# Second experts of an audio tower: routing weights of chunks 2 to 7 spread by DMA, sums turned whole, first products a chunk ahead

## The reference

```python
logits = tokens @ router_w.T
rw, re = top_k(softmax(logits), 2)
rw = rw / maximum(rw.sum(-1, keepdims=True), 1e-12)
combine = zeros((N, E)).at[arange(N)[:, None], re].set(rw)
out = tokens
for e in range(8):
    h = gelu(tokens @ w1[e] + b1[e], approximate=False)
    out = out + combine[:, e:e + 1] * (h @ w2[e] + b2[e])
```

## Time and profile before

| | |
|---|---|
| median of 3 runs | 734.57 us (733.91 to 736.68) |
| the profiled execution | 732.55 us, its span 730.8 us |
| mean granted TensorE clock | 0.954 of full |
| PE busy | 635.5 us (87%) |
| DVE busy | 569.5 us (78%) |
| ACT busy | 502.0 us (69%) |
| POOL busy | 346.1 us (47%) |
| DMA | 24.36 MB, mean 33 GB/s |

### The profile page before, as it was taken

How to read it: one execution, slowest core, us unless ns; L and a number is a source line. 1 busy time by engine, 2 the same in 40 slices (tenths; PEclk the granted TensorE clock), 3 DMA queues, 4 the chain that set the end, 5 groups by cost and what they waited for, 6 DMA issues and landing times.

```text
span 730.8 us, 16309 instructions
## 1 busy us (share of the span) xinstructions
PE 635.5 (87%) x4928; PEld 348.6 (48%) x4928; DVE 569.5 (78%) x1627; ACT 502.0 (69%) x1264; POOL 346.1 (47%) x431
## 2 busy tenths in 40 slices
PE   5527998999999998999999996799888988879896
PEld 5514665665666654222222224555555655554332
DVE  6676787777777784889999989679988888857653
ACT  3747877888888873667777777567777777745542
POOL 1006678778788785433444455625445644320000
PEclk9858999999999998999999998699999999987999
DMA  4030000000000000533333330000000000000011
GB/s 112 1 115 1 1 2 1 0 0 0 0 0 0 0 1 24 185 116 117 118 115 117 117 118 1 2 1 2 0 0 1 0 0 0 1 1 2 15 22 22
DMA packets 22421, 24.36 MB, mean 33 GB/s; under 512 B 12390, under 2 KB 13414, under 8 KB 22118
## 3 DMA queue, kind: packets, MB, share of 16 engines
q1 hardware_dynamic: 20135, 23.31, 10.3%
q10 hardware_dynamic: 2239, 0.49, 0.4%
HBM read 22.48 MB, written 1.31 MB: 33 GB/s over the span
## 4 chain that ended last, share of the span: by engine, by line
PE 54%; DVE 25%; issue 9%; ACT 3%; POOL 2%; DMA 1%; DVEq 0%; SPq 0%; ACTq 0%; POOLq 0%
PE ps L726 8%; PE ps L762 8%; DVE big L1103 5%; PE ps L1581 5%; PE ps L1603 4%; PE ps L720 4%; DVE big L2093 3%; DVE big L1144 2%; PE ps L644 2%; PE ps L1587 2%; PE ps L655 2%; PE ps L708 2%; PE ps L712 2%; DVE big L1053 2%; PE ps L1836 2%
## 5 line engine op out<-in xcount | busy, mean ns | idle before, releaser
L1358 POOL TENSOR_TENSOR big<-big 128x1024 f32<-128x1024 f32 x64 | 119.9, 1895 | 44.1 <-DVE big L1164 44.1
L942 ACT ACTIVATE big<-ps,big 128x255 f32<-128x255 f32 x256 | 117.3, 485 | 11.4 <-DVE big L1158 8.9
L904 ACT ACTIVATE big<-ps,b1s 128x512 f32<-128x512 f32 x128 | 80.8, 683 | 33.3 <-PE ps L644 32.2
L1158 DVE TENSOR_REDUCE big<-ps 128x4 f32<-128x1020 f32 x64 | 75.1, 1213 | 26.6 <-PE ps L720 26.6
L1953 ACT ACTIVATE big<-ps 128x1024 f32<-128x1024 f32 x64 | 65.9, 1030 | 33.9 <-PE ps L1593 31.6
L2093 DVE TENSOR_REDUCE big<-ps 128x4 f32<-128x1020 f32 x64 | 78.1, 1220 | 6.8 <-DVE res L2150 2.5
L726 PE MATMUL ps<-cst,big 128*128 128x128 f32 x512 | 76.7, 283 | 6.3 <-POOL big L1358 2.4
L1170 DVE COPY mid<-ps 128x512 f32<-128x512 f32 x96 | 63.4, 685 | 18.3 <-PE ps L726 15.1
L726 PEld LDWEIGHTS ps<-cst,big 128*128 128x128 f32 x512 | 54.2, 140 | 40.8 <-issue 20.4
L644 PE MATMUL ps<-big,wall 64*128 64x512 f32 x256 | 73.1, 648 | 0.4 <-ACT big L875 0.4
L655 PE MATMUL ps<-big,w2s 128*64 128x512 f32 x256 | 70.8, 631 | 1.7 <-DVE big L1144 1.3
(11 more groups left out here) (277 smaller groups left out, 1310.6 us busy)
## 6 DMA issues: line engine op xcount, KB each, us to landing
mid<-spread_w SPq DMA_DIRECT2D x128, 128.0 KB, 2.9
mid<-in_split_sel SPq DMA_DIRECT2D x1, 1536.0 KB, 7.3
wall<-in_w SPq DMA_DIRECT2D x1, 1280.0 KB, 6.3
out_tokens<-res SPq DMA_DIRECT2D x16, 56.0 KB, 1.6
cst<-in_consts SPq DMA_DIRECT2D x1, 520.5 KB, 4.8
pexp<-in_w_raw SPq DMA_DIRECT2D x1, 512.0 KB, 5.8
w2s<-in_w SPq DMA_DIRECT2D x1, 512.0 KB, 3.2
mid<-in_taps ACTq DMA_DIRECT2D x1, 320.0 KB, 3.8
```

The source lines that it names most:

```text
L904: last = nc.scalar.activation(hid[e % 2][j], H1(e, j), ACT.Relu, bias=b1s[0][:, 2 * e + j:2 * e + j + 1])
L942: last = nc.scalar.activation(e_sb[r % 4][:, jj, tq, 0:NW], S[:, 2 * (r % 2) + jj, tq, 0:NW], ACT.Exp, scale=-1.0, bias=minus[r % 4][:, jj ...
L1158: nc.vector.tensor_reduce(minus[r % 4], S[:, 2 * a:2 * a + 2, :, 0:NW], AX.X, ALU.min).then_inc(s_mx, 1)
L1358: nc.gpsimd.tensor_tensor(e_sb[r % 4], e_sb[r % 4], bc(inverse[r % 4].unsqueeze(3), [P, 2, 2, 256]), ALU.mult).then_inc(s_A, 1)
```

## The change

- The first products run one chunk ahead: `hid` gets a second set of four buffers, PE's list becomes `hidden(c+1, 1)`, [`spread(c, 0)`], `second(c-1, 1)`, `hidden(c+2, 0)`, [`spread(c, 1)`], `sum_turn(c-1)`, `second(c, 0)`, and ACT's list follows it.
- `spread` on PE stays for chunks 0 and 1 only. For the others the combined table of a half (not its bf16 parts) is turned by one PE transpose (`combine_turn`), copied by ACT (`combine_out`), written to DRAM by SP (64 KB) and read back with two DMAs of 512 KB a chunk into `by_dma`, two buffers. `spread(c)` for c from 4 on waits until both weighings of chunk `c - 2` are done. `weigh` then reads both operands from SBUF.
- `sum_turn` is four plain transposes; `finish` adds the two halves, one each in two DVE operations. The tokens are added to `res` beforehand by POOL (`tokens_added`, eight operations of 128x256).
- The exponential of half 1 is a POOL power with base e of 128x16 in place of an ACT exponential (which needed two table loads).
- `combine` is split in `where`, `shares`, `combine` and `split`. Chunk 0 is taken first, then chunks 1 to 3, whose split comes after `weigh(0, 0)`. DVE's order around it changes too: `slot(B // 2, 2)` and `(B // 2, 5)` move behind that split, `rank(4)`, `best(6)` and `weigh(1, 0)` ahead of `slot(B // 2 + 1, 1)`, `rank(5)` and `slot(B // 2 + 1, 2)`.
- SP's stores are written out in place of a loop, each behind a `spread` of a later chunk for chunks 0 to 3.

The core of the diff (indentation cut by twelve):

```diff
+comb_turned = [big[:, 11008 + P * n:11008 + P * n + P] for n in range(2)]
+BY_PE = 2
+by_dma = [pos_t[:, 4 * n:4 * n + 4].rearrange("p k c q -> p k (c q)") for n in range(2)]
+there = [spread_w[2 * n:2 * n + 2].rearrange("c e q -> (c e) q") for n in range(2)]
+COMB_TURNED = lambda n: ps[:, 7 - 2 * n, 0:P]
...
-hid = [mo[:, 512 * n:512 * n + 512] for n in range(4)]
+hid = [mo[:, 512 * n:512 * n + 512] for n in range(4)] + [mid[:, 1024 + 512 * n:1536 + 512 * n] for n in range(4)]
...
+base = tail[:, 0:half]
...
+s_comb, s_cwp, s_cw, s_there = e0.s_comb, e0.s_ctp, e0.s_ct, e0.s_cd
+s_by_dma, s_pre = [sem(f"e1_spread{n}") for n in range(2)], sem("e1_tokens_added")
...
     def weights(d):
...
-        pe.wait_ge(s_c3, d // 4 + 1)
-        if d < 2:
+        pe.wait_ge(s_c3, 1 if d == 0 else 2 if d < 4 else 3)
+        if d == 0:
             pe.wait_ge(s_otr, B)
+        elif d == 2:
+            pe.wait_ge(s_fin, B)
+        elif d == 6:
+            pe.wait_ge(s_cw, CH + 2)
         for k in range(TC):
             last = nc.tensor.transpose(turned_weights(d)[:, P * k:P * k + P], c3[:, TC * d + k].rearrange("p r s -> p (r s)"), ident_b[:])
         last.then_inc(s_ctp, 1)
+    def combine_turn(n):
+        pe.wait_ge(s_comb, CH + n + 1)
+        if n == 0:
+            pe.wait_ge(s_ct, 1)
+        else:
+            pe.wait_ge(s_wgt, GROUPS * BY_PE)
+        nc.tensor.transpose(COMB_TURNED(n), comb_rows[n], ident).then_inc(s_cwp, 1)
     def hidden(c, g):
...
     def spread(c, g):
...
         s = GROUPS * c + g
-        pe.wait_ge(s_ct, 2 if s < 2 else 4 if s < 7 else CH)
+        pe.wait_ge(s_ct, c + 1)
         if s == 0:
             pe.wait_ge(s_lc, 6)
-        if s >= 1:
+        else:
             pe.wait_ge(s_wgt, s)
...
         s = GROUPS * c + g
+        if s == 0:
+            pe.wait_ge(s_ct, 4)
         if g == 0 and c >= 1:
             pe.wait_ge(s_ysb, c)
+        if g == 0:
+            pe.wait_ge(s_ct, 4 if c < 4 else CH)
         pe.wait_ge(s_wgt, s + 1)
...
-            last = nc.tensor.matmul(YT[:, D * k:D * k + D], y_sb[:, P * k:P * k + P], fold[:], start=True, stop=True)
+            last = nc.tensor.transpose(YT[:, P * k:P * k + P], y_sb[:, P * k:P * k + P], ident)
...
     hidden(0, 0)
-    for d in range(2):
-        weights(d)
+    hidden(0, 1)
+    hidden(1, 0)
+    weights(0)
+    hidden(1, 1)
     for c in range(CH):
-        hidden(c, 1)
+        if 1 <= c < CH - 1:
+            hidden(c + 1, 1)
+        if c < BY_PE:
+            spread(c, 0)
         if c == 0:
-            pe.wait_ge(s_fin, B)
-            for d in range(2, 4):
+            combine_turn(0)
+            for d in range(1, 4):
                 weights(d)
-        spread(c, 0)
         if c >= 1:
             second(c - 1, 1)
         if c < 2:
             x_turn(6 + c)
         if c == 3:
-            pe.wait_ge(s_wgt, GROUPS * c + 1)
             for d in range(4, CH):
                 weights(d)
-        if c < CH - 1:
-            hidden(c + 1, 0)
+        if c < CH - 2:
+            hidden(c + 2, 0)
         if c < 2:
             logits(6 + c)
-        spread(c, 1)
+        if c < BY_PE:
+            spread(c, 1)
+        if c == 2:
+            combine_turn(1)
         if c >= 1:
             sum_turn(c - 1)
-        if c == 0:
-            pe.wait_ge(s_ct, 4)
         second(c, 0)
     second(CH - 1, 1)
     sum_turn(CH - 1)
...
         act.wait_ge(s_tr, c + 1)
         nc.scalar.activation(xcol[:, c], ps[:, X_BANK[c]], ACT.Copy).then_inc(s_xc, 1)
-    def gap(n):
...
+    def activate(c, g):
...
+            last = nc.scalar.activation(hid[4 * (c % 2) + 2 * g + n], H1(g, n), ACT.Gelu, bias=b1s[1][:, 2 * g + n:2 * g + n + 1])
+        last.then_inc(s_hid, 1)
     slot(B // 2, 2, ("o",))
...
-    gap(0)
-    for d in range(2):
-        weights(d)
+    gap()
+    activate(0, 0)
+    activate(0, 1)
+    weights(0)
+    activate(1, 0)
     for c in range(CH):
-        for g in range(GROUPS):
...
+        if c < CH - 1:
+            activate(c + 1, 1)
+        if c == 0:
+            weights(1)
+            combine_out(0)
+            for d in range(2, 4):
+                weights(d)
+        if c >= 1:
+            y_out(c - 1)
+        if c < 2:
+            columns_out(6 + c)
+        if c == 3:
+            for d in range(4, CH):
+                weights(d)
+        if c < CH - 2:
+            activate(c + 2, 0)
+        if c == 2:
+            combine_out(1)
     y_out(CH - 1)
...
-    def combine(n):
...
+    def local(first, count):
+        n = first // half
+        return slice(first, first + count), comb[n][:, first - half * n:first - half * n + count], [P, count, E]
+    def where(first, count):
...
+    def combine(first, count):
+        tl, co, shape = local(first, count)
+        for i, dst in ((0, co), (1, pick[:, tl])):
+            link(nc.vector.tensor_tensor(dst, dst, bc(wts[:, 2 + i, tl].unsqueeze(2), shape), ALU.mult))
+        ins = nc.vector.tensor_tensor(co, co, pick[:, tl], ALU.add)
+        if first == 0:
+            link(ins)
+        else:
+            ins.then_inc(s_comb, 1)
+            dve.wait_ge(s_comb, CH + first // half + 1)
+    def split(first, count):
...
-        if n == 0:
+        if first == 0:
             dve.wait_ge(s_pad3, 1)
-        link(nc.vector.tensor_copy(hi, thrice(comb)))
...
     def finish(c):
-        y = YT[:, 0:TC * D].rearrange("p (t d) -> p t d", t=TC)
+        halves = YT.rearrange("p (t n d) -> p n t d", t=TC, n=2)
         tl = slice(TC * c, TC * c + TC)
         dve.wait_ge(s_yt, c + 1)
-        link(nc.vector.tensor_tensor(yy, y, x2[:, tl, 0], ALU.add))
-        nc.vector.tensor_tensor(res[:, tl], res[:, tl], yy, ALU.add).then_inc(s_done, 1)
+        dve.wait_ge(s_pre, c + 1)
+        link(nc.vector.tensor_tensor(yy, halves[:, 0], res[:, tl], ALU.add))
+        nc.vector.tensor_tensor(res[:, tl], yy, halves[:, 1], ALU.add).then_inc(s_done, 1)
     def weigh(c, g):
         s = GROUPS * c + g
         dve.wait_ge(s_hid, s + 1)
-        dve.wait_ge(s_cb, s + 1)
+        if c < BY_PE:
+            dve.wait_ge(s_cb, s + 1)
+        else:
+            dve.wait_ge(s_by_dma[c % 2], 32 * (c // 2))
         if s >= 2:
             dve.wait_ge(s_w2, s - 1)
         for n in range(2):
-            last = nc.vector.tensor_tensor(wgt[2 * g + n], hid[2 * g + n], CB(n), ALU.mult)
+            rows = CB(n) if c < BY_PE else by_dma[c % 2][:, 2 * g + n]
+            last = nc.vector.tensor_tensor(wgt[2 * g + n], hid[4 * (c % 2) + 2 * g + n], rows, ALU.mult)
         last.then_inc(s_wgt, 1)
-    def best(c):
-        logits_out(c)
-        rank(c)
...
     best(3)
     difference(0)
     logits_out(4)
-    combine(0)
+    where(0, TC)
+    shares(0)
+    combine(0, TC)
+    split(0, TC)
     logits_out(5)
     slot(B // 2, 7, ())
+    where(TC, half - TC)
+    combine(TC, half - TC)
+    weigh(0, 0)
+    split(TC, half - TC)
     slot(B // 2, 2, ())
     slot(B // 2, 5, ())
-    weigh(0, 0)
+    weigh(0, 1)
     slot(B // 2, 6, ())
-    slot(B // 2 + 1, 1, ())
     rank(4)
-    weigh(0, 1)
-    slot(B // 2 + 1, 2, ())
-    rank(5)
     best(6)
     weigh(1, 0)
+    slot(B // 2 + 1, 1, ())
+    rank(5)
+    slot(B // 2 + 1, 2, ())
+    weigh(1, 1)
     best(7)
     difference(1)
-    weigh(1, 1)
     finish(0)
-    for c in range(2, CH):
+    weigh(2, 0)
+    where(half, half)
+    shares(1)
+    combine(half, half)
+    weigh(2, 1)
+    finish(1)
+    split(half, half)
+    for c in range(3, CH):
         weigh(c, 0)
-        if c == 2:
-            combine(1)
         weigh(c, 1)
         finish(c - 1)
     finish(CH - 1)
...
+            nc.gpsimd.memset(base, math.e)
             nc.gpsimd.memset(c3, 0.0).then_inc(s_pad3, 1)
...
+    def tokens_added(c):
+        pool.wait_ge(s_nx, 2 * c + 2)
+        tl = slice(TC * c, TC * c + TC)
+        nc.gpsimd.tensor_tensor(res[:, tl], res[:, tl], x2[:, tl, 0], ALU.add).then_inc(s_pre, 1)
+    for c in range(CH - 2):
+        tokens_added(c)
+    pool.wait_ge(s_dv, 2)
+    nc.gpsimd.tensor_tensor(wts[:, 0, half:], base, wts[:, 0, half:], ALU.pow).then_inc(s_ex, 1)
+    for c in range(CH - 2, CH):
+        tokens_added(c)
...
+    def spread(c):
+        n, row = c // (CH // 2), c % (CH // 2)
+        if c >= BY_PE + 2:
+            sp.wait_ge(s_wgt, GROUPS * (c - 1))
+        for j in range(2):
+            rows = there[n].rearrange("(k j c) q -> c j k q", k=2 * GROUPS, j=2)[row, j]
+            sp.dma_start(by_dma[c % 2][D * j:D * j + D], bc(rows.unsqueeze(0), [D, 2 * GROUPS, 512])).then_inc(s_by_dma[c % 2], 16)
+    for n in range(2):
+        sp.wait_ge(s_cw, CH + n + 1)
+        sp.dma_start(there[n].rearrange("(e c) (t q) -> (e c t) q", e=E, t=TC), comb_turned[n]).then_inc(s_there, 16)
+        sp.wait_ge(s_there, 16 * (CH + n + 1))
+        for c in ((2, 3), (4,))[n]:
+            spread(c)
+    store(0)
+    for c in range(5, CH):
+        spread(c)
+        store(c - 4)
+    for c in range(CH - 4, CH):
         store(c)
```

(6 more changed lines are left out.)

62 lines of the change are left out of this document (27 added, 35 removed).

## The result

The changed kernel takes 741.08 us (median of 14 runs, 738.55 to 745.14) against 734.62 for the kernel before on the same chip (14 runs, 732.45 to 737.34): a ratio of 1.0099 [1.008, 1.0118]. It is slower by 1%, where the forecast was 732.2 and the range ended at 737.5. Executions of one kernel differ by some us, so what follows from two profiles alone is rougher than what follows from the medians.

The account below looks back on a forecast made before the run. PE bounds the steady part; before it no engine bounds alone. Steady part -12.3, head +6.5, clock +2.7, POOL +0.6, stores -0.4, walk +0.5 make -2.4 us: median 734.57 to 732.2, range 727.5 to 737.5.

Parts of the forecast that it names:

- 6.0 fits: Spreading transfers of chunks from 2 on: 1 MB lands about 5.2 us after issue, plus 1.0 to issue; hidden.
- The point of decision: Steady part: from 3.8 us of moving a chunk, the transfers rather than PE's 4.8 us list decide.
- rival C: Weighings of chunks 5 to 7 wait for transfers, 6.3 us a chunk: +8, 740; chance 0.17 for slower by over 0.5%.
- M: Landmark: start of the first weighing of chunk 2, at 681.17 us in the kernel before.
- The steady part without transfers: From M to DVE's last operation: 32.2 us against 44.5, -12.3, with transfers hidden and 4.80 us a chunk.
- The first stretch: From M through weighing, combining, turns and second products with bias: 5.5 us.
- round 3: Steady part: sixteen turns of 1.02 us added to the four other parts, 5.9 us.
- H: Landmark set after measuring: start of the first first product, 658.59 us before, 660.63 after.
- +6.5: Head, ahead of M: the new list order moves M from 681.2 to 687.7 us, without clock falls.
- The clock's +2.7: Head: PE's rests of 2.7 and 4 us bring clock falls, +2.3 and +0.8; M at 690.4.
- Rival D: Head: the second clock fall lasts to 687.5 or longer; -0.6 to 0, about 734.2; chance 0.10.
- the +0.6 of the forecast: Behind POOL's power: its last two token sums can hold up the combining, +0.6, between 0 and 1.5 us.

## Why the prediction was wrong

**The step that failed is the transfers': "I split in 3.5 of moving and 1.5 to 1.7 of latency", "6.0 fits", hidden.** 1 MB takes about 5.6 us of moving (an estimate, 1.049 MB by the 187 GB/s of the row above, stores included), not 3.5, and the twelve DMAs, two for each MB, landed after 8.3 us at the median, not 5.2. The point of decision was put rightly, at 3.8 us of moving; the number was taken from the wrong row. The earlier trace rows are one load in which each byte is read once; the spreads read the same 8 KB for 64 partitions, and sixteen of that kind stood in the earlier trace rows with 6.3 us for 1 MB. (What of the pattern makes them slow is shown for the run length alone, 187 against 224 GB/s; rows that are read only once were not tried. The load itself took 6.3 to 8.5 us in the later profiles, so its single 6.3 was at the low end.) The text gave the spreads to rival C at 0.17 with the objection that they "were issued one by one"; two issues a chunk moved at 187 GB/s, those sixteen at 167, so the objection was void. The rule that followed was right: "from above 5.3 us of landing each further us costs 3" makes 9.0 us of a landing of 8.3, and M to the end was 8.7 us shorter with a quarter of the bytes. About 2 of these are the low clock behind the wait of 2.81 us at 725.77 (from the weighing of chunk 6 to DVE's end it is 13.4 against 11.2 us). Chunk 4 waits too, 3.8 us, which C did not name: from the end of its combining to the landing it took 11.4 us where 8.5 stood.

C said +8 on the forecast, 740; the median is 741.08. That it comes so close is in part luck: by the medians the transfers are worth 6.3 us, by the run with a quarter of the bytes alone, and 6.9 with the order mended as well, and the rest comes from the head.

**The steady part without transfers** was right in kind: with a quarter of the bytes 33.9 us from M to the end, forecast 32.2. A round is 4.93, forecast 4.80, since a plain turn in its row costs 0.58 us and not 0.45. The first stretch, to the end of the second products, is 6.6 instead of 5.5; round 3 is as forecast.

**The head.** Its sequence came as written: rests of 2.71 and 4.83 us where "2.7" and "4" stood, the first ended by the weight parts, the second by the last scaling. Without the falls the walk holds: 34.5 less 4.0 and 1.1 for the two falls is 29.4 us from H to M, where +6.5 made 29.1. DVE's list alone brought 7.6 us of it back, the second fall with it. The clock's +2.7 was too small, and its two terms, +2.3 and +0.8, add up to 3.1. The first fall cost 1.1, the second 4.0. I had let it end by 684; it began at 684.2 and held until 697 in that execution. The terms together make 5.1, 2.4 more than the sum took, and H to M lies 2.7 above the forecast (34.5 against 31.8). Rival D, a longer second fall, thus occurred as well; it had put this at 1.8 to 2.4 us.

**The reason for the fall** was only half right. The rests of 2.71 and 4.83 us end with the clock low in the changed kernel, but standing still is not needed: twenty-four bf16 products with 24 rows in place of the rest end with it low too, nine or five f32 ones with 64 rows do not. The two kinds differ in rows and in type, and no run parts the two; and two f32 ones ahead of sum_turn(0) did not hold it. What decides stays open. (The Trainium skill, TensorE: Matmul & The Clock Gate, Part 1, speaks of waits that let the clock fall; the runs agree for the waits of 2.71 and 4.83 us, and the light products show a fall without one.)

**POOL.** The power took 2.91 us, forecast 2.8. Its sums slowed three of DVE's steps: the last scaling 1.23 instead of 0.60, the weighing at M 1.84 instead of 1.28, and finding places behind it 1.22 instead of 0.61, against the +0.6 of the forecast. The first is on the path, since x_turn(7) waits for it; for the others the chain of waits runs through PE and ACT in this profile, so 0.6 may stand by chance. The scaling is of a kind that the prediction had not named: it has one operand in SBUF of full size and small ones beside it. **The stores**: 4.7 instead of 5.1 us at the end, the -0.4 of the forecast.

Of the signs that were to prove it wrong, "weighings that wait for DMA" is the one that came. What stays open: 2 us of the difference between the two profiles lie ahead of H. H stands anywhere between 656.3 and 663.4 in the profiles of this study, with the granted clock differing between 20 and 60, 280 and 300 and 440 and 480 us. It stands at 659.7 on average in the fifteen profiles with the changed head and at 657.3 in the four with the old one, so the changed code may well have a part in it; that was not tried.

## What to carry to other kernels

Work taken off the engine that bounds is worth only what its substitute delivers in a round: 1 MB of spreads bought 1.06 us of PE in a round of 4.9 us, and needed 5.6 us to move; the trace had that kind of transfer elsewhere. Price a transfer by the row that has its pattern (rows read again for many partitions, run length), not by one of its size. With four chunks sent instead of six and two rounds for each buffer, the same slow transfers were hidden. When a list is rewritten, look for the operation on which the other engine's next burst hangs (here one scaling behind two weighings): an edit of a few lines in DVE's order was worth 7 us.

## What the runs showed of the hardware

- Small stores beside busy spreads land late: 5.5 us (56 KB) in the changed kernel, 1.7 in the run with a quarter of the bytes. The spreads themselves hardly gain when the stores go (8.2 to 7.5 us).
- Spreads read in 2 KB runs moved 187 GB/s at a DMA share of 0.98, in 8 KB runs 224 at 1.00.
- 6.0 us of bf16 products with 24 rows, without a gap, ended at the low clock; f32 products with 64 rows in the same place kept it full. Five of these took 4.9 us off the changed kernel's 741.
- Nine f32 products of 512 columns that all used rows 0 to 63 took 0.89 us each; the kernel's pairs, one on rows 0 to 63 and one on 64 to 127, take 1.06 for two. (The Trainium skill, TensorE: Matmul & The Clock Gate, Part 3, says that small products on different rows run side by side; the trace agrees.)
- A POOL sum of 128 x 256 doubled DVE's scaling of 128 x 128 beside it (1.23 and 1.41 for two instead of 0.60). With POOL's sums moved behind the last scaling, in the changed kernel's list with four chunks by DMA, it took 0.61 again.
